# A macaron block with two attentions: the rows of negated maxima of the second attention, their low parts issued by ScalarE

## What is computed

```python
q, k, v = jnp.split(x @ W_qkv + b_qkv, 3, axis=-1)        # 16 heads of D = 8
idx = jnp.arange(T)                                       # T = 1024
alibi = jnp.minimum(idx[None, :] - idx[:, None], 0)
bias = slopes[:, None, None] * alibi
scores = jnp.einsum('bhtd,bhsd->bhts', q, k) / sqrt(D) + bias[None]
w = jax.nn.softmax(scores, axis=-1)
y = jnp.einsum('bhts,bhsd->bhtd', w, v)
```

## Time and profile before

| | |
|---|---|
| median of three runs | 1372.04 us |
| profiled execution, its own time | 1382.75 us |
| its span from first to last instruction | 1381.0 us |
| TensorE busy in the span | 1150.9 us, 83% |
| VectorE | 864.0 us, 63% |
| ScalarE | 692.1 us, 50% |
| GpSimd | 523.8 us, 38% |
| mean granted clock of TensorE | 0.912 of full |
| second attention, from its first to its last score matmul | 773.7 to 1162 us |

### The profile page before, as it was taken

The page is one execution under the profiler, slowest core; times in us unless marked ns, Lnnn a source line. Parts: engine busy times, 40 slices in busy tenths (PEclk is TensorE's granted clock), DMA queues, the critical chain, the costliest instruction groups (busy, mean ns, idle before and its releaser), DMA issues. The chain is left out here.

```text
span 1381.0 us, 18918 instructions
## 1 busy us (share of the span) xinstructions
PE 1150.9 (83%) x6221; PEld 573.6 (42%) x6221; DVE 864.0 (63%) x1895; ACT 692.1 (50%) x847; POOL 523.8 (38%) x517
## 2 busy tenths in 40 slices
PE   1599999999999846579836899999999998576885
PEld 0344444444444842369721222222222222335774
DVE  7456576666766656623357888888888880674231
ACT  3477777777777142012230366666666666221221
POOL 1056566665657102268600121221231121024774
PEclk9799999999999957789965799999999999697997
DMA  1000010101010106047568202211210000412662
GB/s 58 1 6 23 21 33 22 31 22 36 22 31 18 32 3 206 14 106 185 99 140 188 38 1 47 47 19 28 47 35 13 1 1 5 148 31 49 155 156 47
DMA packets 58385, 74.71 MB, mean 54 GB/s; under 512 B 21942, under 2 KB 46646, under 8 KB 56502
## 3 DMA queue, kind: packets, MB, share of 16 engines
q1 hardware_dynamic: 44028, 64.68, 18.1%
q0 software_dynamic: 11264, 8.92, 4.5%
q10 hardware_dynamic: 3024, 0.22, 0.2%
HBM read 60.51 MB, written 12.98 MB: 53 GB/s over the span
## 5 line engine op out<-in xcount | busy, mean ns | idle before, releaser
L1600 DVE TENSOR_REDUCE at_MX<-psum 128x1 f32<-128x512 f32 x512 | 318.1, 682 | 60.7 <-PE psum L1677 60.6
L1571 ACT ACTIVATE at_PR<-psum 128x1024 f32<-128x1024 f32 x256 | 251.5, 1022 | 178.7 <-PE psum L1692 178.6
L1677 PE MATMUL psum<-at_KS,at_QS 120*128 120x512 bf16 x512 | 205.8, 404 | 7.7 <-DMA at_KS<-at_parts_dram 6.7
L1543 POOL TENSOR_TENSOR at_PR<-at_PR,at_FAC 128x512 f32<-128x512 f32 x64 | 81.0, 1266 | 345.4 <-ACT at_PR L1571 345.4
L1692 PE MATMUL psum<-at_QS,at_KS 122*128 122x512 bf16 x512 | 192.3, 386 | 5.1 <-DMA at_QS<-at_MR 4.6
L522 ACT ACTIVATE PR<-psum 128x1024 f32<-128x1024 f32 x144 | 140.9, 1026 | 84.7 <-PE psum L761 79.7
L761 PE MATMUL psum<-Q,K 64*128 64x512 f32 (+3 forms) x768 | 145.3, 508 | 3.1 <-ACT PR L522 3.1
L527 ACT ACTIVATE PR<-PR 128x1024 f32<-128x1024 f32 x144 | 144.5, 1062 | 0.0
L1708 PE MATMUL psum<-at_PR,at_VG 128*32 128x512 f32 x1024 | 136.2, 604 | 9.5 <-ACT at_OTS L1565 4.7
L773 PE MATMUL psum<-PR,V 128*64 128x512 f32 (+3 forms) x768 | 139.7, 495 | 0.1
L1324 PE MATMUL psum<-moe_XGT,moe_WE 128*128 128x256 f32 x512 | 124.9, 400 | 7.1 <-ACT moe_XGT L1085 6.8
(11 more groups left out here) (220 smaller groups left out, 1526.2 us busy)
## 6 DMA issues: line engine op xcount, KB each, us to landing
moe_WE<-in_c_We SPq DMA_DIRECT2D x32, 768.0 KB, 4.3
XB<-at_r_dram SPq DMA_DIRECT2D x32, 256.0 KB, 3.9
at_QS<-at_parts_dram SPq DMA_DIRECT2D x24, 192.0 KB
at_KS<-in_c_krows SPq DMA_DIRECT2D x8, 384.0 KB
at_parts_dram<-at_SPL SPq DMA_DIRECT2D x12, 256.0 KB, 2.5
moe_rows_dram<-XNS SPq DMA_DIRECT2D x2, 1152.0 KB, 10.1
at_KS<-at_parts_dram SPq DMA_DIRECT2D x16, 128.0 KB
at_QS<-at_MR SPq DMA_DIRECT2D x128, 1.0 KB
```

The lines of the kernel that those rows point to most:

```text
L1543: pool.tensor_tensor(pr, pr, FAC[:, 4 * (s // 2):4 * (s // 2) + 4, :], ALU.mult).then_inc(z.factored, 1)
L1571: act.activation(PR[:, gu % PRS, 2 * r:2 * r + 2, :].rearrange("p h n -> p (h n)"), g.psum[:, 2 * r * BANK:(2 * r + 2) * BANK], ACT.Exp).t ...
L1600: dve.tensor_reduce(MX[:, 4 * (r // 2 % 4) + r // 8, r % 2:r % 2 + 1], bank(("max", c))[:, :], AX, ALU.max).then_inc(z.reduced, 1)
L1677: pe.matmul(bank(("max", c))[:, :], QS[0:MROW, t, h, I * P:(I + 1) * P], KS[0:MROW, t, h, khalf * BANK:(khalf + 1) * BANK], start=True, st ...
```

## The change

A function `maxima_rows(eng, hs, k)` replaces SyncE's `maxima(hs)`. It waits for the split of half `hs` and issues the four DMAs of part `k` on the engine that is given. SyncE issues those of the high part (`k` = 0), where it issued all eight. ScalarE issues those of the low part (`k` = 1): for half 0 ahead of its loop, and for each half `h` from 1 to 15 in its loop, at unit 8 (`h` - 1) + 5, ahead of that unit's exponentials. The wait of the score matmuls and the bytes that are written are as before.

```diff
--- before.py
+++ after.py
@@ -1440,6 +1440,14 @@
             hs, k = c // 32, c % 32
             return hs // 2, hs // 2 % STACKS, (k // 2) % 4, 4 * (hs % 2) + k // 8, k % 2
 
+        def maxima_rows(eng, hs, k):
+
+            t, half = hs // 2 % STACKS, hs % 2
+            eng.wait_ge(z.msplit, hs + 1)
+            for h in range(4):
+                eng.dma_start(QS[MROW + k:MROW + k + 1, t, h, half * BANK:(half + 1) * BANK].rearrange("o (i n) -> o i n", n=P),
+                              MR[4 * h:4 * h + 4, k, :]).then_inc(z.mrows, 16)
+
         def diagonals(gu):
 
             s, _, half, J = place(gu)
@@ -1481,15 +1489,6 @@
                     for k in range(PARTS):
                         sp.dma_start(parts_dram[side, b, :, k].rearrange("q d h n -> (d h) q n"),
                                      SPL[:, n, k, :]).then_inc(y.kept[b], 16)
-
-                def maxima(hs):
-
-                    t, half = hs // 2 % STACKS, hs % 2
-                    sp.wait_ge(z.msplit, hs + 1)
-                    for k in range(2):
-                        for h in range(4):
-                            sp.dma_start(QS[MROW + k:MROW + k + 1, t, h, half * BANK:(half + 1) * BANK].rearrange("o (i n) -> o i n", n=P),
-                                         MR[4 * h:4 * h + 4, k, :]).then_inc(z.mrows, 16)
 
                 sp.dma_start(W[:, :], g.i["c_Wqkv1"]).then_inc(y.loaded, 16)
                 sp.dma_start(bq[:, :], g.i["c_bqk"]).then_inc(y.loaded, 16)
@@ -1515,7 +1514,7 @@
                         sp.wait_ge(z.multiplied, UNITS * (s - 2))
                         bias_rows(s)
                         part_rows(s)
-                    maxima(hs)
+                    maxima_rows(sp, hs, 0)
 
             @block.gpsimd
             def _(pool):
@@ -1564,7 +1563,10 @@
                     wait(act, z.oturned, hs - 1)
                     act.activation(OTS[:, hs % 2, :], O[:, :], ACT.Copy).then_inc(z.taken, 1)
 
+                maxima_rows(act, 0, 1)
                 for gu in range(STEPS1 * UNITS):
+                    if gu % BT == 5 and gu // BT + 1 < HALVES:
+                        maxima_rows(act, gu // BT + 1, 1)
                     for r in range(2):
                         act.wait_ge(z.scored, 2 * gu + r + 1)
                         wait(act, z.multiplied, gu - PRS + 1)
```

## The result

The changed kernel takes 1440.47 us (median of 4 runs, 1436.95 to 1442.21) against 1371.65 us (1370.16 to 1375.13) in the same session. The ratio is 1.0498, with a 95% interval of 1.0481 to 1.0515: 4.98% slower, 68.8 us between the medians. The forecast was 1432 us, +60, in a range of 1405 to 1452.

The account below looks back on a forecast made before the run. TensorE was taken to bound the second attention. Stalls of 46 and 2.1 us less gains of 0.5 and 0.9 gave +47; the clock's 13 made +60: 1443 us profiled, 1432 at the median, range 1405 to 1452.

Parts of the forecast that it names:

- The bound on the gain: Second attention: faster writing of maxima rows can save at most the 4.6 us that TensorE's scores wait for them.
- The last half's 1.34 us: TensorE's wait for maxima rows before the last half, predicted to go; kept only if TensorE still arrives as early.
- the two small waits: TensorE's two waits for maxima rows away from the first and last halves, 0.5 us together, predicted to go.
- The first half's 0.9 us: Gain taken from TensorE's 2.72 us wait for rows before the first half, with bounds of 0 and 2.7 us.
- The stop: ScalarE's wait and four issues ahead of unit 5's exponential stall TensorE 3.3 us per half, 46 us over 14 halves.
- The wait alone: ScalarE's wait for the split costs 2.2 us at unit 5, using all 2.0 us of slack before any issue.
- Issue holds nothing up: Rival: ScalarE's DMA issues cost its own work nothing; TensorE waits 0.2 us per half; no change, 1372.4 us; chance 0.03.
- faster: Rival: unit 5's exponential delay stays in ScalarE's idle time, all waits for rows go; -4.6 us, 1367.4; chance 0.04.
- blocked wholly: Rival: two issuers block each other, ScalarE's four issues take 4.9 us, stall 5.1 us; +99, 1471 us; chance 0.03.
- The clock: TensorE's clock drops behind some of 15 stalls: 8 falls taken, 1.7 us each, 13 us.
- clock at every half: Rival: TensorE's clock falls behind all 15 stalls, costing 25 us; +72, 1444 us, up to +76, 1448; chance 0.19.
- The sum's base: Profiled execution of 1382.75 us lay 10.7 us above the runs' median; that difference was carried over, 1443 becoming 1432 us.

Follow-up runs that it names:

- the experiment without issues: Kernel before, with ScalarE only waiting for the split maxima ahead of unit 5 and issuing no DMAs; 1384.91 against 1382.49 us, ratio 1.0013.
- the run with work in the stops: Changed kernel with 12 more 512-column matmuls on TensorE ahead of unit 6's first scores in 14 halves; 1429.38 us, ratio 1.0337 to the kernel before.

## Why the prediction was right

**The bound on the gain.** Right: 4.6 us in four places. The last half's 1.34 us and the two small waits went. The first half's 0.9 us did not come.

**The stop.** Right in mechanism and near in size: 3.17 us in the mean where 3.3 was the sum. ScalarE's four issues took 2.84 to 3.05 us, mostly 2.86, not 3.1: one takes 0.72 us in the median. My upper bound had two of them at 0.91 us, which stands in no row of an issue; the rows had 0.87. The 15 stops make 47.5 us; the prediction had 46 for 14 and 3.4 for the last.

**The wait alone, and the rivals.** By the experiment without issues the wait uses the slack and stops TensorE for 0.2 us, as the rows said (915.53 + 1.02 - 916.37). "Issue holds nothing up" and "faster" are out, since each row moved to ScalarE makes the stop longer; "blocked wholly" is out by the stop of 3.17 us where it had 5.1. The Trainium skill's sentence (DMA: Bandwidth & Descriptors, Issuing engines are not separate DMA queues) that a second engine only saves issue time agrees: SyncE's eight of 4.88 us became four of 2.49, and nothing else was won. Its "usually small" doesn't hold for these rows, as the prediction said: 4.88 us of issues against 1.1 behind them.

**The clock.** The term that was mis-sized, by half. I took 8 falls of 1.7 us, 13 us; the 8 was a choice between none and 15, not read from rows. There were 11; 4 of 3.4 us and 7 of about 5.5 us behind the stop, at half speed: (4 x 3.4 + 7 x 5.5) / 2 = 26 us. The row I priced a fall by the earlier trace rows had its fall after the stop; where it came well inside one the low time was longer. The pair of halves above (2.6 us for one such fall) and the run with work in the stops (22 us) bear out the size. My rival "clock at every half" had 25 us, nearer to what was lost than the forecast's 13, but by 15 falls of 1.7 us, which isn't what happened.

**The sum, mended.** 47.5 + 26 + 1.4 (first half) - 1.3 (last half) - 0.5 = 73.1 us, against 73.2 in the profiles. The agreement to 0.1 us is partly luck: without the first half's 1.4 it is 71.7, where the stretch between the first and last score matmul grew by 71.2, and the 0.7 us more lie ahead of the first score. The timed runs have 68.8; the profiled execution is the slowest of its four, by 1.7 us above the median, and at the lowest mean granted clock (0.897, against 0.898, 0.899 and 0.902), and its first wait was a long one. The remaining 1 to 3 us I can't place. Against the profiles the forecast of +60 is 13 us short, and that is the clock's term: of the others, the shorter stops (1.9 us less than the sum had) and the first half (2.3 us more) nearly cancel. So the stops' 47 us came out by mechanism, and the nearness of the total within them by some luck.

**The sum's base.** I carried the 10.7 us by which the profiled execution lay above the median over as they were. It was right to keep them out of the change: they lie ahead of the attention, which started 12.3 us later in that profile, as in the four of the slower chip.

## What to carry to other kernels

Before a DMA is moved to an engine that computes, look at who waits for the next instruction of that engine, and count its slack from the moment at which the DMA's data is ready: 2.0 us of slack were used up by the wait before the first issue. The same issues one unit later cost 8 us in place of 68, and two of them, one ahead of each exponential, nothing that could be measured. And a stop of TensorE in dense work can cost more than its length: in the kernels with three and four rows on ScalarE the clock fell at 23 of 30 stops of 2.1 to 3.3 us.

## What the runs showed of the hardware

- Four 1 KB DMAs issued on ScalarE beside four on SyncE take 2.86 us in most halves (2.84 to 3.05), and SyncE's 2.5; one issue on ScalarE's queue takes 0.58 us at least, 0.72 in the median and 1.19 at most. A single issue at a time took 0.58 to 0.60 us, beside SyncE's too. In two halves of the kernel with the issues one unit later, four in a row took 0.58 each; why there isn't known.
- ScalarE's DMA issue can run beside the activation ahead of it: at 867.00 us it started 0.58 us before that activation's end.
- Stops of 1.46 to 2.05 us were followed by a fall of TensorE's clock once in 15, of 2.1 to 2.5 us in 12 of 15, of 3.1 to 3.3 us in 11 of 15. The low time was 3.4 us, or 6.8 in the eight stops where it began 0.66 to 1.42 us ahead of the stop's end; where it began 0.03 to 0.51 us ahead of it, in four stops, it was 3.4.
- With 168 matmuls more on TensorE, in the stops, the kernel was 22 us faster than the changed one.
